# Swapping a group's router logits one period sooner and splitting its routing steps, in an attention and expert kernel

## The reference, cut to what matters

```python
# x: 64 sequences x 128 tokens x 256; ctx the same; 16 heads of 16; 8 experts, the best 2 are used
h = layernorm(x)
Q, K, V = h @ Wq + bq, ctx @ Wk + bk, ctx @ Wv + bv          # split into heads
x = x + (softmax(Q K^T / 4) V) @ Wo + bo
n = layernorm(x)
probs = softmax(n @ router)                                  # 8 per token
w, idx = top_k(probs, 2); w = softmax(w)
x = x + sum over the 2 experts of w * ((silu(n @ gating[e]) * (n @ up[e])) @ down[e])
```

## Time and profile before

| | |
|---|---|
| median of 3 runs | 1359.26 us (1358.9 to 1364.22) |
| the profiled execution's own time | 1358.88 us |
| its span | 1357.1 us |
| TensorE busy | 1300.3 us (96%) |
| VectorE busy | 673.5 us (50%) |
| ScalarE busy | 725.4 us (53%) |
| GpSimd busy | 423.9 us (31%) |
| first stage | from about 22 to 590 us |

### The profile page before, as it was taken

The page is one execution under the profiler, slowest core; times in us unless marked ns, Lnnn a source line. Parts: engine busy times, 40 slices in busy tenths (PEclk is TensorE's granted clock), DMA queues, the critical chain, the costliest instruction groups (busy, mean ns, idle before and its releaser), DMA issues.

```text
span 1357.1 us, 37763 instructions
## 1 busy us (share of the span) xinstructions
PE 1300.3 (96%) x13790; PEld 1122.3 (83%) x13791; DVE 673.5 (50%) x1974; ACT 725.4 (53%) x1106; POOL 423.9 (31%) x353
## 2 busy tenths in 40 slices
PE   6999999999999999889999999999999999999996
PEld 3777676676667667679999999999999999999996
DVE  3667776777777776744454333333333333333332
ACT  3566656666666665566654444444444444444443
POOL 3112223333333333214454322222222222222222
PEclk9999999999999999999999999999999999999999
DMA  4434444444444433214343333333333323233332
GB/s 140 118 112 118 128 131 133 134 137 141 140 129 136 124 111 95 74 44 82 76 84 76 51 48 47 47 51 47 48 50 47 47 47 51 47 48 49 47 47 35
DMA packets 98716, 112.52 MB, mean 83 GB/s; under 512 B 13072, under 2 KB 85776, under 8 KB 98608
## 3 DMA queue, kind: packets, MB, share of 16 engines
q1 hardware_dynamic: 71120, 72.87, 19.3%
q0 software_dynamic: 26400, 37.09, 16.1%
q10 hardware_dynamic: 1088, 1.05, 0.2%
HBM read 48.72 MB, written 45.46 MB: 69 GB/s over the span
## 4 chain that ended last, share of the span: by engine, by line
PE 57%; DVE 2%; DMA 1%; issue 1%; POOL 1%; ACT 0%; DVEq 0%; POOLq 0%; ACTq 0%
PE banks L477 53%; PE banks L681 2%; DMA out<-x_sb,token 1%; DVE row_max L985 1%; POOL sorted_x L400 1%; PE banks L520 0%; PE banks L506 0%; PE banks L532 0%; DMA sorted_x<-xn,slots_now 0%; PE banks L543 0%; DVE attn L1001 0%; PE banks L569 0%; DVE x L1006 0%; POOL out L430 0%; PE banks L549 0%
## 5 line engine op out<-in xcount | busy, mean ns | idle before, releaser
L430 POOL DMA_INDIRECT out<-x_sb,token x135 | 210.2, 1557 | 495.4 <-DVE x_sb L1259 426.4
L1246 DVE TENSOR_TENSOR qT<-qT,banks 128x512 f32<-128x512 f32 x135 | 92.8, 687 | 437.0 <-PE banks L477 437.0
L843 ACT ACTIVATE qT<-banks 128x512 f32<-128x512 f32 x135 | 80.6, 597 | 365.3 <-PE banks L477 365.1
L477 PE MATMUL banks<-xnT,kT 128*128 128x128 f32 x2176 | 265.3, 275 | 0.0
L477 PE MATMUL banks<-xnT,probs 128*128 128x128 f32 x2144 | 261.6, 275 | 0.8 <-DVE xnT L1241 0.8
L477 PEld LDWEIGHTS banks<-xnT,kT 128*128 128x128 f32 x2176 | 258.7, 192 | 3.8 <-issue 0.4
L477 PEld LDWEIGHTS banks<-xnT,probs 128*128 128x128 f32 x2144 | 254.7, 192 | 4.7 <-DVE xnT L1241 1.2
L477 PE MATMUL banks<-down_sb,qT 128*128 x1080 | 255.6, 380 | 0.8 <-DVE x_sb L1259 0.8
L477 PEld LDWEIGHTS banks<-down_sb,qT 128*128 128x128 f32 x1080 | 194.9, 191 | 22.0 <-issue 1.2
L400 POOL DMA_INDIRECT sorted_x<-xn,slots_now x128 | 124.5, 972 | 182.6 <-DVE slots_now L1075 122.0
L985 DVE TENSOR_REDUCE row_max<-banks 128x16 f32<-128x2048 f32 x64 | 146.7, 2292 | 67.8 <-PE banks L506 65.2
(11 more groups left out here) (161 smaller groups left out, 1665.2 us busy)
## 6 DMA issues: line engine op xcount, KB each, us to landing
xn<-sorted_x SPq DMA_DIRECT2D x136, 130.5 KB
x_sb<-in_x SPq DMA_DIRECT2D x16, 512.0 KB, 3.9
ctxT_sb<-in_ctx SPq DMA_DIRECT2D x16, 512.0 KB, 4.1
heads<-kT SPq DMA_DIRECT2D x128, 64.0 KB, 2.4
heads<-qT SPq DMA_DIRECT2D x128, 64.0 KB, 2.3
out<-x SPq DMA_DIRECT2D x16, 512.0 KB
gate_sb<-_L_ffn_kernel_gating_EDF SPq DMA_DIRECT2D x8, 512.0 KB, 4.7
up_sb<-in_L_ffn_kernel_up_EDF SPq DMA_DIRECT2D x8, 512.0 KB, 4.5
```

The lines of the kernel that those rows point to most:

```text
L430: pool.indirect_dma_start(out=out[:, :], out_offset=bass.IndirectOffsetOnAxis(ap=token[:, v, :], axis=0), in_=ys[:, u, :], in_offset=None, ...
L477: last = nc.tensor.matmul(dst, lhsT, rhs, start=(i == 0), stop=(i == len(pairs) - 1))
L843: nc.scalar.activation(gatedT[:, u, :], score[:, u, :], ACT.Silu).then_inc(s_silu, 1)
L1246: nc.vector.tensor_tensor(fusedT[:, u, :], gatedT[:, u, :], score[:, 2 + u, :], ALU.mult).then_inc(s_fuse, 1)
```

## The change

In the second period the logits are swapped right behind `swap_max`, into columns P to 2P of the bank that holds the swapped maxima. `route_shift` follows `take_max_off` directly, `router_exp` moves from the third period to the second, and `norm_swapped` in the second period now waits for `route_shift`, since it writes that bank. In the third period `route_second` stands ahead of `row_maxes`, four of the steps of `route_third` between `row_maxes` and `take_max_off`, and `second_shift` behind `take_max_off`; the last three steps of `route_third` become `route_fourth`, behind `second_shift`. The wait for attn ahead of `scores_swapped` stays only where the bank is written. In the last group `values` stands ahead of `attend`. In group 13 `early_table(0)`, the count of chosen tokens, stands ahead of `first_shift`. No instruction is added or dropped.

```diff
@@ PE, stage_a
+                    if not nxt and b < 3:
+                        values(u, b + 1, other_bank(i, 1))
                     if one:
                         attend(i - 1, (b + 1) % 2, other_bank(i, 2))
                     swap_max(i, other_bank(i, 3))
+                    if b == 1 and prev2:
+                        swap_logits(g - 2, other_bank(i, 3)[:, P:2 * P])
...
-                    if b < 3 or nxt:
+                    if nxt:
                         wait(pe, s_piece_c, min(5 + i, SEQS))
                         values(u if b < 3 else 1 - u, (b + 1) % GROUP, other_bank(i, 1))
...
                     if b < 2 and nxt and g > 0:
                         wait(pe, s_less, i * 2 + 2)
+                        if b == 1 and prev2:
+                            wait(pe, s_route, (g - 2) * ROUTE_STEPS + SHIFTED)
                         norm_swapped(g + 1, b, other_bank(i, 3))
...
-                    if prev2:
+                    if b == 0 and prev2:
                         wait(pe, s_attn, i)
-                    if b == 0 and prev2:
...
-                    if b == 1 and prev2:
-                        swap_logits(g - 2, other_bank(i, 2))
                     if b == 2 and prev2:
+                        wait(pe, s_attn, i)
                         places(g - 2, other_bank(i, 2))
                     if b == 3 and g == EARLY_GROUPS + 1:
+                        wait(pe, s_attn, i)
@@ ACT, stage_a
-                    if b == 2 and prev2:
-                        router_exp(g - 2)
...
+                    if b == 1 and prev2:
+                        router_exp(g - 2)
                     softmax_exp(i)
@@ DVE, route_third
                 steps.then(nc.vector.tensor_tensor(picks[:, 1], tied[:], over_experts(xn2[:, u, :, RANKS + 1]), ALU.is_equal))
+
+            def route_fourth(g, u):
+                steps = Steps(dve, s_route, g * ROUTE_STEPS, SHIFTED + 11)
+                steps.wait()
                 steps.done(nc.vector.tensor_tensor(chosen[:], picks[:, 0], picks[:, 1], ALU.add))
@@ DVE, stage_a
+                    if b == 2 and prev2:
+                        route_second(g - 2, u)
                     row_maxes(i)
+                    if b == 2 and prev2:
+                        route_third(g - 2, u)
+                    if b == 3 and far:
+                        first_stats(g + 2, (0, 1))
+                    if b == 1 and prev2:
+                        wait(dve, s_logit, g - 1)
+                    take_max_off(i, other_bank(i, 3))
+                    if b == 1 and prev2:
+                        route_shift(g - 2, other_bank(i, 3)[:, P:2 * P])
                     if b == 2 and prev:
                         second_shift(g - 1)
                     if b == 2 and prev2:
-                        route_second(g - 2, u)
-                    if b == 3 and far:
-                        first_stats(g + 2, (0, 1))
-                    take_max_off(i, other_bank(i, 3))
-                    if b == 2 and prev2:
-                        route_third(g - 2, u)
+                        route_fourth(g - 2, u)
...
-                    if b == 1 and prev2:
-                        route_shift(g - 2, other_bank(i, 2))
...
+                    if b == 3 and g == EARLY_GROUPS + 1:
+                        early_table(0, other_bank(i, 2))
                     if b == 3 and far:
                         first_shift(g + 2)
-                    if b == 3 and g == EARLY_GROUPS + 1:
-                        early_table(0, other_bank(i, 2))
```

More of the change, by code:

```diff
@@ L1278, in behind_tile @@
                     route_third(GROUPS - 2, 0)
+                    route_fourth(GROUPS - 2, 0)
                 if t == 9:
@@ L1288, in behind_tile @@
                     route_third(GROUPS - 1, 1)
+                    route_fourth(GROUPS - 1, 1)
                 if t == 15:
```

## The result

The changed kernel takes **1394.04 us** (median of 4 runs, 1392.95 to 1394.68). The kernel before took 1361.38 on the same chip (median of 4, 1358.9 to 1364.22). The ratio is 1.0226 [1.02, 1.0253]: slower by 33 us at the medians (31 by the ratio), and by 35.4 between the two profiled spans.

What follows compares the result with a forecast made beforehand. TensorE, busy nearly all the span, was taken as the bound, so only its waits count. Third periods +14.5, group 13 -0.7 and clock +6.8 gave +20.6 on 1358.88 us: forecast 1380 us, range 1363 to 1387.

Steps and rivals of the forecast that it cites:

- Third period, the chain: Groups 3 to 14: x_bo holds the first routing step, delaying shift, norm and `places`; +1.21 us each, +14.5 in all.
- Rival 1: Third period: the first routing step isn't held; 1355 us, or 1348 if the clock's falls end too; chance 0.16.
- Rival 4: Third period: the hold is no bound, but VectorE overflows ahead of row_max; 1363 us at most; chance 0.06.
- Clock: Third and fourth periods: TensorE's longer pause brings four more falls of the clock, +6.8 us; bounds none and eight more.
- rival 3: Third period: the routing step is held and the clock falls in all twelve groups; 1387 us; chance 0.14 with beyond.
- Second period: Earlier logits swap and added routing steps are hidden by existing waits: 0 us, bounds -0.1 and +0.3 each, 14 times.
- Group 13: The count goes ahead of `first_shift`, shortening TensorE's wait of 1.66 us: -0.7 us, once.
- Group 2: Its third period has no rows to write and an earlier x_bo: 0 us, bounds 0 and +1.2.
- Last group: `values` ahead of `attend` wins in the second period, VectorE takes most back in the third: 0 us, bounds -1 and +0.5.
- The idea that the shift's place is the loss: Third period: the shift behind four routing steps and q_less makes the norm late, and `places` 1.21 us later.

Runs made afterwards that it cites:

- g1: The changed kernel as it is, on a chip of the experiments: 1509.86 us, ratio 1.0133 to the kernel before.
- g3: The changed kernel with GpSimd's root2 and x_bo waiting for the third period's scores: 1529.65 us, ratio 1.027 to the kernel before.
- e3: The changed kernel with x_bo waiting until q_less of the third period is ready: 1490.01 us, ratio 1.0033 to the kernel before.
- h2: The kernel before with root2 and x_bo waiting for the third period's scores, and only the shift moved behind q_less: 1509.74 us, ratio 1.0168.
- g2: The kernel before with root2 and x_bo waiting for the third period's scores: 1492.33 us, ratio 1.0017 to the kernel before.
- h1: The changed kernel with root2 and x_bo waiting for the third period's scores, and unused matmuls filling TensorE's two pauses: 1499.68 us, ratio 1.0083.
- g4: The changed kernel with root2 and x_bo waiting for the third period's scores, and the shift directly behind row_max again: 1486.47 us, ratio 0.998.
- f4: The kernel before with one unused matmul of 384 columns in each of TensorE's two pauses: 1490.61 us, ratio 1.0001.
- e2: The kernel before with only the shift moved behind q_less in the third period: 1506.45 us, ratio 1.0119.

## Why the prediction was right and wrong

**Third period, the chain: right in each step.** The first routing step was held (1.89 us, taken as 1.83), the shift was bare behind q_less, and the norm started 5.67 behind row_max's start, forecast 5.6. The residual and the swap started within 0.1 of its end, and `places` came 1.29 later instead of 1.21. The term was +14.5; idle time grew by 14.9. The pause from the end of `values` to `places` is 459.66 to 463.32, 3.66, forecast 3.60. Rival 1, a routing step that isn't held, fell on the twelve rows of L1046 (mean 1895 ns), and on g1 and g3: the step is short where x_bo is elsewhere, and long again where x_bo is put back. Rival 4, VectorE overflowing ahead of the third period's row_max, is not seen: row_max starts 1.41 us into the period (454.32 - 452.91), against 1.48 before. On the other chips row_max is late in every other group of g1, but through the held first step of `route_second`, which no rival had named.

The rule by which rival 1 was judged is that of the Trainium skill, "SBUF — State Buffer", section on the two separate sides: a VectorE instruction with two SBUF inputs and a GpSimd instruction that reads SBUF exclude each other, and the later one waits until the first is over. These rows agree with it: TENSOR_TENSOR on 32 columns took 1.89, SCALAR_TENSOR_TENSOR on 4 columns 2.11 in e3, and row_max from PSUM 2.29 as ever beside x_bo.

**Clock: the step that failed.** The prediction took "the middle, four more" falls, at 1.71 us, for +6.8. The clock fell in all twelve groups: eight more, the case of rival 3. Measured are +15.9 us in TensorE's busy time. By the full-clock group of the earlier trace rows, the twelve groups' busy time holds 115.45 + 111.38 - 12 x (8.87 + 8.23) = 21.6 us over full clock, 1.8 for each. The four before held 108.39 + 102.51 - 12 x 17.10 = 5.7, 1.4 each. So the falls also cost more than before, and the term was short by 9.1 us. Two readings in it failed. One is the number: the term halved between its bounds, where the argument had already said that the pause grows by half in every group, so that no reason spoke for four more rather than eight. (Nor did the rows of before say that it would be all: in h2 the norm is a whole us later than in g2, and the clock falls in seven groups of twelve.) The other is the price. The 1.71 compares whole periods, and 0.33 of it is a longer wait: group 4 had 11.41 - 9.33 = 2.08 us idle, group 11 1.75. The clock's own share there was 1.38, and after the change it is 1.8. So the bound of 13.7 for eight more was too low as well. The h1 and g3 pair shows the cause: with the same chain and the pauses filled, the clock is full, and the third and fourth periods are 17.8 us shorter.

**Second period:** taken as 0, bounds -0.1 to +0.3; measured +0.06 each, 0.7 in all. **Group 13:** -0.7 taken, -0.8 measured. **Group 2:** taken as 0, bounds 0 to +1.2; measured +2.0, since there too the third period is 1.27 longer and the clock falls behind it. The prediction had let this group off because it has no rows to write, though the shift moves there as in the others. The same holds for group 1 (+0.6), which it didn't count. **Last group:** 0 taken, +0.4 measured, inside the bounds, with the third period taking back more than the second won, since the norm starts 3.97 behind row_max's start there instead of 3.52. The sum was 20.6 and 35.4 was measured. Of the 14.8 between them, 9.1 are the clock, 2.6 groups 1 and 2, 1.9 group 0 and the start, and the rest small differences in the other terms. The clock term alone at rival 3's 13.7 would have given that rival's 1387, the range's end; what is missing beyond it, 7 us, is the dearer falls (2.2), groups 1 and 2 (2.6), and group 0 and the start (1.9).

**The idea that the shift's place is the loss** came out of the experiments stronger than it was written: without it the change is a small gain (0.997, 0.9985, 0.998), and with it alone the loss on the experiments' chips is there (1.0119, 1.0124; the whole change 1.0133), or the larger part of it (with x_bo pinned, 22 of 37 us, h2). None of these runs was made on the chip of the result, so for its 33 us the cause is shown by its own rows and by the pinned kernels of another chip.

Left open: why the second period takes 17 to 18 us on four chips and 8.3 on the first, with the same program. The records show only that VectorE and ScalarE wait, put down to "remote". Open too is what decides whether the clock falls in a group: e3 and g1 differ by 0.13 us in the norm's start and by five falls.

## What to carry to other kernels

When steps are spread over idle places, ask of each instruction that moves back who waits for it on the other engines: the shift is 0.15 us of work, and it opens a chain of 2.07 us on ScalarE that ends at TensorE. Steps that nobody waits for go behind the head of such a chain, not ahead of it, even where the head's place is one that is held by GpSimd (g4's shift was held for 1.19 us and g4 was still 43 us under g3). And price a longer pause of TensorE twice, as idle time and as what the matmuls after it take at half clock; here the two were about equal (14.9 and 15.9 us in the changed kernel, 16.5 and 17.2 in g3).

## What the hardware showed that I had not expected

- A pause of 2.50 us, 1.6 longer than before, was followed by some 7 us at the 1.2 GHz level in a group where TensorE was busy nearly all the rest of the time. Matmuls whose results nobody reads, put into the pause, took this away (h1) and cost nothing where there was nothing to take away (f4, 1.0001).
- The clock falls in every other group in g1 (fourth periods of 9.63 and 8.24 us in two neighbouring groups with the same instructions), and in six and seven of twelve in e2 and h2. The groups without a fall aren't free in g1: their third periods are some 0.6 longer. A mean over groups hides both.
- A GpSimd instruction of 2.36 us holds one VectorE instruction with two SBUF inputs whatever its size (4 or 32 columns), until 0.02 to 0.06 us behind its own end. It does so wherever the two meet: behind row_max in the changed kernel, behind q_less in e3, ahead of row_max in g1.
- The same program takes 1361 us on one chip and 1486 to 1490 on four others.
